# Row-wise logits between gates, products that nothing reads in three waits, and a first expert that starts on three row tiles

## What is computed

```python
r1 = bi_wkv(x, fside, fside, w1, u1, cond)        # two decaying scans, a ratio, times sigmoid(x)
inp, decay, gate = silu(r1@W_in), sigmoid(r1@W_decay+bias), sigmoid(r1@W_gate)
state = decay * state + (1 - decay) * inp          # scan over tokens
x2 = x + (gate * state) @ W_out + b_out
r2 = bi_wkv(x2, fside, fside, w2, u2, cond)
probs = softmax(r2 @ Wg)                           # 8 experts
gate_vals, expert = top_k(probs, 2)                # at most 640 tokens for each expert, in order
out = x2 + sum_k gate_vals_k * (relu(r2[tokens] @ w1[e]) @ w2[e])
```

## Time and profile before

| what | us |
|---|---|
| three runs | 1118.91, 1120.66 (median), 1121.45 |
| the profiled execution, its own time | 1115.98 |
| its span, first to last instruction | 1113.8 |
| PE busy | 1035.3 (93%) |
| DVE busy | 636.6 (57%) |
| ACT busy | 519.9 (47%) |
| POOL busy | 281.6 (25%) |
| mean granted clock of TensorE | 0.978 |

### The profile page before, as it was taken

How to read it: one execution, slowest core, us unless ns; L and a number is a source line. 1 busy time by engine, 2 the same in 40 slices (tenths; PEclk the granted TensorE clock), 3 DMA queues, 4 the chain that set the end, 5 groups by cost and what they waited for, 6 DMA issues and landing times.

```text
span 1113.8 us, 17234 instructions
## 1 busy us (share of the span) xinstructions
PE 1035.3 (93%) x5042; PEld 814.0 (73%) x5043; DVE 636.6 (57%) x931; ACT 519.9 (47%) x836; POOL 281.6 (25%) x231
## 2 busy tenths in 40 slices
PE   3599997999997999999999999999999999999994
PEld 2334543454465899999998999898887888999893
DVE  5899999999983333343334333555564444344552
ACT  6776775677643233343334333445454334333541
POOL 4665758634855000020002000301102003000202
PEclk9999998999988999999999999999999999999997
DMA  6991432224625211162126222735536226222621
GB/s 211 330 306 29 114 84 88 57 57 114 203 64 181 82 71 64 62 168 75 74 75 170 75 75 75 196 125 179 158 113 217 75 75 160 76 79 85 174 75 23
DMA packets 67104, 131.34 MB, mean 118 GB/s; under 512 B 4966, under 2 KB 6026, under 8 KB 67080
## 3 DMA queue, kind: packets, MB, share of 16 engines
q1 hardware_dynamic: 53856, 105.25, 27.2%
q0 software_dynamic: 13008, 25.52, 11.6%
q10 hardware_dynamic: 216, 0.28, 0.1%
HBM read 90.66 MB, written 35.22 MB: 113 GB/s over the span
## 4 chain that ended last, share of the span: by engine, by line
PE 64%; issue 1%; DVE 1%; DVEq 0%; POOL 0%; ACT 0%; ACTq 0%; POOLq 0%
PE ps_y L1608 11%; PE ps_y L1609 11%; PE ps_y L1610 11%; PE ps_h L1588 10%; PE ps_h L1590 10%; PE ps_h L1589 10%; PE ps_t L1558 1%; POOL out_dram L1537 0%; DVE y L1813 0%; DVEq L1664 0%; DVE hl L1790 0%; ACT y L1736 0%; ACT w1h L1690 0%; DVE w1l L1750 0%; DVE gate L1775 0%
## 5 line engine op out<-in xcount | busy, mean ns | idle before, releaser
L1588 PE MATMUL ps_h<-xh,w1h 128*128 128x320 f32 (+4 forms) x768 | 244.5, 318 | 6.7 <-issue 6.4
L1590 PE MATMUL ps_h<-xh,w1l 128*128 128x320 f32 (+4 forms) x768 | 240.7, 313 | 0.1
L1589 PE MATMUL ps_h<-xl,w1h 128*128 128x320 f32 (+4 forms) x768 | 240.8, 313 | 0.0
L1537 POOL DMA_INDIRECT out_dram<-y,token x40 | 63.6, 1590 | 638.3 <-DVE y L1813 413.4
L1790 DVE SCALAR_TENSOR_TENSOR hl<-ps_h,hh 128x320 fp32r<-128x320 f32 (+1 forms) x192 | 107.2, 558 | 189.4 <-ACT hh L1716 189.2
L1608 PE MATMUL ps_y<-w2h,hh 128*128 128x512 f32 x528 | 207.2, 392 | 3.2 <-issue 1.7
L1609 PE MATMUL ps_y<-w2h,hl 128*128 128x512 f32 x528 | 206.3, 391 | 0.0
L1610 PE MATMUL ps_y<-w2l,hh 128*128 128x512 f32 x528 | 206.1, 390 | 0.0
L1716 ACT ACTIVATE hh<-ps_h 128x320 fp32r<-128x320 f32 (+1 forms) x192 | 94.2, 491 | 232.7 <-PE ps_h L1590 232.6
L1753 DVE TENSOR_TENSOR w2l<-raw,w2h 128x512 fp32r<-128x512 f32 x127 | 87.8, 692 | 199.0 <-ACT w2h L1693 199.0
L1693 ACT ACTIVATE w2h<-raw 128x512 fp32r x127 | 80.1, 631 | 212.1 <-PE ps_y L1610 212.1
(11 more groups left out here) (207 smaller groups left out, 1160.7 us busy)
## 6 DMA issues: line engine op xcount, KB each, us to landing
raw<-in_L_ffn_w_dram SPq DMA_DIRECT2D x64, 1024.0 KB
slots<-r_rows SPq DMA_DIRECT2D x8, 1302.5 KB, 20.8
rows<-slots SPq DMA_DIRECT2D x7, 1302.5 KB, 7.9
rows<-in_x_dram SPq DMA_DIRECT2D x4, 1024.0 KB, 5.3
sums_even<-eukv POOLq DMA_DIRECT2D x8, 512.0 KB, 6.4
sums_odd<-eukv POOLq DMA_DIRECT2D x8, 512.0 KB, 6.0
out_dram<-rows SPq DMA_DIRECT2D x4, 1024.0 KB, 5.3
f_rows<-in_fside_BxSxS_dram SPq DMA_DIRECT2D x3, 1024.0 KB, 6.7
```

The costliest lines, as they stand in the source:

```text
L1588: nc.tensor.matmul(o, w1h[:, j, dt, :], xh[:, dt, lo:hi], start=(dt == 0), stop=False)
L1589: nc.tensor.matmul(o, w1h[:, j, dt, :], xl[:, dt, lo:hi], start=False, stop=False)
L1590: last = nc.tensor.matmul(o, w1l[:, j, dt, :], xh[:, dt, lo:hi], start=False, stop=(dt == CT - 1))
```

## The change

1. **Logits row by row.** `logits(b)` becomes `logits(b, i)`, one row tile of four narrow products, and the 4 calls of each sample are set between other work: sample 0 between `x2_row`, `gate(1, 3)` and `r2_row`; sample 1 between the turns of x and r2; sample 2 from before `gate(3, 11)` to before `r2_row(2, 1)`.
2. **Products that nothing reads.** `unread(bank, count)` issues `count` float32 products of 512 columns into a PSUM bank whose contents are not used any more: 3 ahead of `project(1)`, 3 ahead of `gate(2, 0)`, and 1 and 2 ahead of `project_tile(0)`.
3. **The first expert begins on three row tiles.** The semaphores of `xh` and `xl` now count two for each expert. For the first expert the first count comes after row tile 2 (three tiles cover slots 0 to 383), the second after tile 4. TensorE's wait moves from ahead of the loop over q into `up` of the even hidden tile, behind the branches on the width: half k = 0 waits for the first count, anything else for the second. These waits are issued in every round q of every expert.

```diff
-        def logits(b):
-            pe.wait_ge(s_r2, b + 1)
-            if b >= 1:
-                pe.wait_ge(s_dest, b)
-            for i in range(TT):
-                for ct in range(CT):
-                    last = nc.tensor.matmul(ps_logit[:, i, :], sig[:, ct, i * P:(i + 1) * P], wg[:, ct, :],
-                                            start=(ct == 0), stop=(ct == CT - 1))
-            last.then_inc(s_logit, 1)
+        def logits(b, i):
+            if i == 0:
+                pe.wait_ge(s_r2, b + 1)
+                if b >= 1:
+                    pe.wait_ge(s_dest, b)
+            for ct in range(CT):
+                last = nc.tensor.matmul(ps_logit[:, i, :], sig[:, ct, i * P:(i + 1) * P], wg[:, ct, :],
+                                        start=(ct == 0), stop=(ct == CT - 1))
+            if i == TT - 1:
+                last.then_inc(s_logit, 1)
+        def unread(bank, count):
+            for _ in range(count):
+                nc.tensor.matmul(bank, wm[:, 3, 0, 0:P], wm[:, 3, 0, :], start=True, stop=True)
...
         x2_row(0, 2)
-        logits(0)
+        logits(0, 0)
         x2_row(0, 3)
+        logits(0, 1)
         gate(1, 3)
+        logits(0, 2)
         r2_row(0, 0)
+        logits(0, 3)
...
         transpose_f(3, 2)
+        pe.wait_ge(s_gates, CT + 2)
+        unread(bank(0), 3)
         project(1)
         transpose_f(3, 3)
+        pe.wait_ge(s_ev_r2, TT)
+        unread(ps_to[:], 3)
         gate(2, 0)
...
         r2_row(1, 0)
+        logits(1, 0)
         transpose_x(3, 0)
         r2_row(1, 1)
+        logits(1, 1)
         transpose_x(3, 1)
+        logits(1, 2)
         transpose_x(3, 2)
         r2_row(1, 2)
-        logits(1)
+        logits(1, 3)
         transpose_x(3, 3)
...
         gate(3, 10)
+        logits(2, 0)
         gate(3, 11)
         r2_row(2, 0)
-        logits(2)
+        logits(2, 1)
+        logits(2, 2)
+        pe.wait_ge(s_gates, CT * (B - 1) + 2)
+        unread(bank(0), 1)
+        logits(2, 3)
         r2_row(2, 1)
+        unread(bank(0), 2)
         project_tile(0)
...
+    FIRST_PART = -(-HALF // P)
...
-        def up(hidden, j, count):
+        def up(hidden, j, count, e=None):
...
                 for k in range(2 if wide else 1):
+                    if e is not None:
+                        pe.wait_ge(s_cur_h, 2 * e + (1 if wide and k == 0 else 2))
+                        pe.wait_ge(s_cur_l, 2 * e + (1 if wide and k == 0 else 2))
...
             count = pe.value_load(counts[0:1, bass.ds(e, 1)], min_val=1, max_val=CAP)
-            pe.wait_ge(s_cur_h, e + 1)
-            pe.wait_ge(s_cur_l, e + 1)
...
-                up(at, 0, count)
+                up(at, 0, count, e)
...
             a.activation(xh[:, :, i * P:(i + 1) * P], first_turned(i), ACT.Copy).then_inc(s_xh, 1)
-        act.sem_inc(s_cur_h, 1)
+            if i in (FIRST_PART - 1, ST - 1):
+                act.wait_ge(s_xh, i + 1)
+                act.sem_inc(s_cur_h, 1)
...
-        dve.wait_ge(s_h0, 1)
-        dve.wait_ge(s_xl, ST)
-        dve.sem_inc(s_cur_l, 1)
+            if i == FIRST_PART - 1:
+                dve.wait_ge(s_h0, 1)
+            if i in (FIRST_PART - 1, ST - 1):
+                dve.wait_ge(s_xl, i + 1)
+                dve.sem_inc(s_cur_l, 1)
```

More of the change, by code:

```diff
@@ L1724, in body @@
                                     act.wait_ge(s_xh, ST * (e + 2))
-                                    a.activation(xh[:], next_xh[:], ACT.Copy).then_inc(s_cur_h, 1)
+                                    a.activation(xh[:], next_xh[:], ACT.Copy).then_inc(s_cur_h, 2)
                                     split(e, c, j)
@@ L1796, in body @@
                                     dve.wait_ge(s_xl, ST * (e + 2))
-                                    v.tensor_copy(xl[:], next_xl[:]).then_inc(s_cur_l, 1)
+                                    v.tensor_copy(xl[:], next_xl[:]).then_inc(s_cur_l, 2)
                                     dve.wait_ge(s_next, 16 * (e + 1))
```

## The result

The changed kernel took 1122.23 us (median of 15 runs, 1120.77 to 1125.72), the kernel before beside it 1119.39 (1116.07 to 1122.24). The ratio is 1.0031 [1.0021, 1.0041]: 3.5 us slower, where 5.8 us faster was forecast. The profiled execution of after took 1122.23 us (span 1120.0), as its median.

The account below looks back on a forecast made before the run. DVE and TensorE were both taken as nearly full in phase one, TensorE alone counting after it. Routing 3.7 plus first expert 2.1 made 5.8 us, off the median 1120.66 giving 1114.9; 8 in 10 for 1110.8 to 1120.8.

Parts of the forecast that it names:

- sample 1's logits: Logits between turns of x and r2: 0.8 us from filled waits plus half of 2.0 for the clock, together 1.8.
- Sample 0's logits: Logits spread over one gate and two row turns, clock already 1.00: zero gain, from -0.3 to +0.5 us.
- Ahead of `project(1)`: Three products inside a 3.52 us wait; `project(1)` 1.7 us shorter, the next wait longer: zero, from 0 to +0.5.
- Ahead of `gate(2, 0)`: Products fill 2.6 of a 5.8 us wait, so the gate tile runs faster: 1.9 us gained, ends 0 and 2.5.
- theory B: Logits' new order alone: VectorE sets sample 2's stretch, 74 us or more against 73.0; time within 0.1% or slower.
- the third rival: Clock falls behind sample 1's waits and logits as before: only 3.0 us gained, time 1117.7; chance 0.15.
- Ahead of `project_tile(0)`: Unread products keep the clock up between sample 2's logits and this tile: 0.6 us gained; ends +1.0 gained, 2.6 lost.
- The first expert: Start on three row tiles: first product 1.6 us earlier, plus 0.5 for the clock, together 2.1 us.
- the branches, which overlap the splitting: First expert's start: load of the count and branches run during the splitting, first product near 360.75, 1.6 us gained.
- the 0.5 us for the clock: First expert's first products: with 1.7 us idle the clock may stay up, saving up to 1.3 us; 0.5 taken.
- the last sentence: Signs of error, among them a branch of the first round that takes longer than before.
- The waits in every round: 256 added waits over 64 rounds, 26 us if nothing hid them: taken as zero, from 0 to +26.

Follow-up runs that it names:

- before with 14 products: Kernel before with 14 instead of 38 wide products that nothing reads ahead of the first expert's transposes: 1120.12 us, ratio 1.0017.
- before with the tests turned round: Kernel before with the branches in `up` testing for the wider half first, so the widest code comes first: ratio to before 1.0028.
- routing with 22 products: Kernel before plus row-wise logits and unread products, with 22 instead of 38 wide products ahead of the first expert: ratio to before 1.0002.
- The unread products alone: Kernel before plus only the unread products in three waits, logits in one block, 34 of 38 wide products in a loop: ratio 1.0019.
- the order alone: Kernel before plus only the row-by-row order of the logits, no unread products, old start of the first expert: ratio 1.0003.
- the kernel with the 57 narrow products: Kernel before plus 57 bf16 products of 8 columns at the end of routing, 114 instructions more: 1124.04 us, ratio 1.0040.

## Why the prediction was wrong, step by step

Two steps failed. The forecast had the branches to the first expert's code as work that overlaps the splitting, and nothing for the place of that code; and it had a gain at sample 1's logits that no stretch shows. The other steps were right in kind, at their forecast size or under it.

Where both kernels of a pair have short branches ahead of the first product, the runs give four differences for routing (+0.02, -0.15, -0.20, -0.27%) and five for part three (+0.10, 0.00, -0.07, -0.09, -0.16%), each uncertain by some 0.18; in some pairs the number of wide products differs too. The means are -0.15 and -0.04%: 1.7 us for the 3.7 forecast, give or take about one, and 0.5 for the 2.1, which can't be told from nothing. The fourteen traces say where. Seven have the old routing (before and its kin), seven the new. Mean us (standard deviation) between DVE's first products with the gates of samples 0 to 3 and sample 3's last `dest`, and the total of half clock at each place:

```
stretch             old routing    new routing    forecast
gate 0 to gate 1    73.4 (1.0)     72.8 (1.0)      0
gate 1 to gate 2    67.7 (1.0)     66.6 (1.6)     -1.9
gate 2 to gate 3    73.0 (0.9)     74.1 (0.8)     -1.8
gate 3 to dest      27.2 (0.8)     26.6 (0.2)     -0.6
clock at 0.50 near  old, us of fall              new
176 us              3.4 in 4 of 7                0 in 7
196 us              6.8 in 7                     0 in 2, 3.4 in 3, 6.8 in 2
250 us              3.4 in 4, 6.8 in 3           3.4 in 2, 6.8 in 5
316 us              6.8 in 6, 3.4 in 1           0 in 7
340 us              6.8 in 5, 10.2 in 2          10.2 in 7
```

*Sample 0's logits* (zero): I read from one trace that the clock stays at 1.00 there. It was that trace's luck. In the eight others with this block the clock fell right behind it, at 130 to 133 us, for 6.8 us in five and 3.4 in three; a gate tile that ordinarily takes 3.67 us took 5.55 in before with 14 products:

```profile
127.97 4.60 PE L604 MATMUL ps_small<-wg,sig 128*128 128x8 f32 x32
...
133.32 5.55 PE L516 MATMUL ps_mm<-ratios,wm 128*128 128x512 f32 x8
```

With the rows between gates it fell in four traces of eight, for 3.4 us each. The 0.6 us of the first stretch can come from this; the forecast put it at nothing.

*Ahead of `project(1)`* (zero): right, the clock no longer falls and the time goes into the next wait.

*Ahead of `gate(2, 0)`* (1.9): the mechanism was right, the size was not. With 3.2 us idle the fall is gone in two traces, where the stretch takes 64.4 us, halved in three (66.1 to 67.3), and whole in two (68.2 and 68.3). Mean 1.1.

*Sample 1's logits* (1.8): this step failed, both its halves. I took 0.8 us for small waits that the rows fill, and 1.0 for a clock that falls less. All engines from gate 2 to gate 3: the old order (before with the tests turned round), then the new one (routing with 22 products), each with a fall of 6.8 us in the stretch, then the old order with a fall of 3.4 (before with 14 products):

```profile
239.40:313.30 73.90, 72.08 (x260) 39.59 (x258) 68.06 (x86) 50.79 (x66) 47.50 (x34) 0.95 0.44 129
```

```profile
241.70:315.80 74.10, 72.04 (x263) 39.21 (x262) 70.36 (x87) 50.43 (x65) 47.52 (x34) 0.95 0.45 129
```

```profile
242.50:314.80 72.30, 70.50 (x260) 38.21 (x258) 70.20 (x86) 50.95 (x66) 47.51 (x34) 0.98 0.45 132
```

At an equal fall the new order changes neither the length (73.9 and 74.1) nor TensorE's idle time (1.8 and 2.1): what the rows fill comes back as the 2.06 us wait for ACT's copy. The length goes with the fall. With 6.8 us of it the stretch takes 73.9 to 74.0 in four traces of the old order and 73.8 to 74.2 in six of the new; with 3.4 it takes 72.3 in five of the old, 73.0 in one of the new and 75.6 in after, of which below. The mean of the new routing is longer by 1.0 mostly because its traces have the long fall more often (five of seven, against three). The unread products alone, in the old order, also take 74.0. So theory B of the order alone isn't borne out either: its 74.1 comes with a fall of 6.8 us. The fall near 250 us stood in all seventeen traces, as the third rival had it; no wide product stands near it.

DVE's busy time is no sign that DVE is the bound there: it is 68.06 and 70.20 in two traces of the same routing code, and the one with more is the shorter. What DVE's waits gave up (9.1 to 3.3 us) did not come back as time. The profiled execution of after stands by itself: 75.5 us long with a fall of 3.4, and DVE busy in 74.8 of them, because some of DVE's instructions ran three to eight times as long, while POOL worked; DVE from 272 to 312 us by form, before and then after:

```profile
L1175 DVE TENSOR_SCALAR sums_even<-sums_even,den_min 128x512 f32<-128x512 f32 x2 | 1.1, 606 | 0.0
...
L1286 DVE TENSOR_TENSOR carry<-carry,sel_sum 128x8 bf16<-128x8 bf16 x1 | 0.2, 158 | 0.0
```

```profile
L1197 DVE TENSOR_SCALAR sums_even<-sums_even,den_min 128x512 f32<-128x512 f32 x2 | 3.6, 1862 | 0.0
...
L1308 DVE TENSOR_TENSOR carry<-carry,sel_sum 128x8 bf16<-128x8 bf16 x1 | 1.3, 1274 | 0.0
```

Five other traces of the new order show 606 to 609 and 156 to 160 ns for these two forms, so I count it as that execution's chance and not as the change's cost; that POOL is the reason wasn't tested.

*Ahead of `project_tile(0)`* (0.6): right, 0.6, and the fall there is gone in all seven.

*The end of routing.* The forecast said nothing of it. The fall near 340 us is 10.2 us long in all traces of the new routing and 6.8 in five of seven of the old. What its 3.4 us cost isn't separated; it lies behind waits of TensorE for DVE.

*The first expert* (2.1): "the branches, which overlap the splitting" is the step that failed. They overlap it when their target's code is there. As made, it was not: the third branch took 3184 ns instead of 208, and the second `up` needed a block more. The worth of the place is 1.5 to 2.8 us in the profiles (13.5, 14.6 and 15.0 against 12.0, 12.3 and 12.2 with the same edits). In the times it is 4.0 [2.2, 5.8] for the whole change, 0.3 for routing and -0.6 for part three, these two uncertain by some 2 and with fewer wide products on one side: a mean of 1.2 us, give or take about one. So the slow branch and its cause are shown; that it makes up all of the whole change's 3.5 us is not.

With the code in place the first product starts 1.6 us earlier behind the turns, as forecast (1.36 to 2.01 us behind them in four kernels, 3.12 to 3.31 in four without part three), but the end of the block sets what follows: 12.2 us in the mean of the four kernels with part three against 12.4 in the four without, a gain of 0.2. The three row tiles themselves bought nothing there: in all four the fifth low part was ready when the first product started, and only with the tests turned round did it start 0.4 and 0.6 us sooner than that. And the 0.5 us for the clock went the other way: between the first product and the third `hl` it stood at 0.50 for 6.5 to 7.0 us with part three, 2.8 to 6.8 without. I had priced the work that the edits add to the path and not the room they take in the code; the last sentence named a longer branch as a sign of error, and gave it no chance.

The Trainium skill, "Runtime: NRT & Kernel Launch", Instruction fetch mechanics, has this rule: code comes in blocks of 256 instructions, ahead of need only in a straight line, and a taken branch to a block that isn't held waits for its fetch. The traces agree, with packets of 16 KB and 0.7 to 6.3 us for such a branch in place of 0.2. A rival of this kind was missing: the 3.2 us of the slow branch in after make it about 3 us slower than the forecast's own sum.

*The waits in every round* (zero): nearly right. TensorE's waits from 362 us in after:

```profile
PE ps_h L1616 <- issue: 9.4, 6, 5.2
```

Of the 9.4 us, 5.23 and 2.72 lie at the first expert's start; 1.4 are left for all rounds, where before has 0.9 (6.4 less 3.31 and 2.17). From the third `hl` to the last `y`, six kernels with part three take 726.5 to 727.4 us, mean 726.8, seven without it (none with the tests turned round) 725.5 to 726.5, mean 726.0: 0.8 us, against a bound of 26.

*Sum.* Stages: routing -1.3 (-1.1 + 1.0 - 0.6, and -0.6 at sample 0's), first expert +2.4, rounds +0.8, or +1.9; the runs say +3.5 [2.3, 4.6]. The rest is within what profiled executions differ by; I can't place it, and the cause of these 1.6 us stays open. The +1.0 in this sum comes mostly from where the falls lay in the traces and from after's own slow instructions.

## What to carry to other kernels

Where an engine jumps between variants of its code, count instructions as a cost of their own, in the compiled program: what stands ahead of a jump decides whether its target's block is there. Here 45 instructions more, with the same products, went with 4.0 us [2.2, 5.8]; in two smaller pairs the traces show 1.5 and 2.3 us of it and the times don't. Before such an edit is judged, put the code back to its place (a loop in place of unrolled filler does it) and measure both. And don't build a forecast on the falls of the clock in one trace: the same code has them elsewhere, and longer or shorter, in the next. Take several, and compare a stretch at equal falls.

## What the runs showed of the hardware

- A compare and branch of TensorE's sequencer took 0.21 us, and 0.7 to 6.3 us where its target had to be fetched. The third one was short with the target up to 21 instructions behind before's place and slow from 30 on. Straight code over the end of the block, 23 instructions behind that place, was late too, by 0.5 to 2.1 us. The last packets of the start begin at 372 to 382 us; in the rounds all seventeen traces together show only one more, at 780 us, in the kernel with the 57 narrow products.
- At 316 us the clock stayed at 1.00 in all seven traces with the new routing (in after 1.23 us idle behind the products), and fell in the seven of the old. Behind `logits(0)` in a block it fell in eight traces of nine, row by row in four of eight. At 196 us, behind as many wide products and 3.2 us of idleness, it still fell in five of seven.
- Between 95 and 345 us falls came in lengths of 3.4, 6.8 or 10.2 us, and not in the same places in each trace. From gate 2 to gate 3 a fall longer by 3.4 us cost 1.7 us of time (72.3 and 74.0). Sample 3's last `dest` started between 338.9 and 343.1 us in seven traces with the same routing code. That spread is as large as the gain that was forecast.
